# Re-slotting the work beside a feed-forward, an in-place residual, an early high band and a DMA broadcast

## What is computed

```
low = x
for 2 levels: l = dwconv(low, h_filter)[:, ::2]; h = dwconv(low, g_filter)[:, ::2]; keep h; low = l
low = linear_attention(low, 16 heads)      # q = k = elu(h)+1, v = h; num = q (k^T v), den = q . sum(k) + 1e-6
for 2 levels back: low = dwconv(repeat2(low), h_synth) + dwconv(repeat2(h), g_synth)
y = layer_norm(x + low, gamma, beta);  x1 = layernorm(x + y)
```

## Time and profile before

| what | us |
|---|---|
| median of 3 runs | 1297.83 |
| the profiled execution | 1299.54 |
| its span, first to last instruction | 1297.7 |
| prologue, to the first gate matmul | 144.4 |
| iterations 0 to 2 (with analysis) | 452.6 |
| iteration 3 | 144.5 |
| iterations 4 to 6 | 421.9 |
| iteration 7, to the last matmul | 128.0 |
| behind the last matmul | 6.3 |

### The profile page before, as it was taken

The page is one execution under the profiler, slowest core; times in us unless marked ns, Lnnn a source line. Parts: engine busy times, 40 slices in busy tenths (PEclk is TensorE's granted clock), DMA queues, the critical chain, the costliest instruction groups (busy, mean ns, idle before and its releaser), DMA issues.

```text
span 1297.7 us, 19451 instructions
## 1 busy us (share of the span) xinstructions
PE 1245.1 (96%) x6000; PEld 641.1 (49%) x6000; DVE 979.8 (76%) x1921; ACT 688.3 (53%) x1427; POOL 363.7 (28%) x794
## 2 busy tenths in 40 slices
PE   8979899989999899989999999999999999999998
PEld 6858454445444444445544444444444444444443
DVE  7878699977999599994998479955997389945231
ACT  6753563467545773467634664466444663466332
POOL 0022332144131441234330441234131433043101
PEclk9998899999999999999999999999999999999999
DMA  8980520017000240004100130014000400010000
GB/s 257 257 210 17 155 91 25 9 44 234 16 33 6 73 142 17 26 26 140 64 34 1 59 129 25 17 34 145 16 32 19 151 25 32 0 57 10 25 9 33
DMA packets 47269, 87.36 MB, mean 67 GB/s; under 512 B 8400, under 2 KB 24016, under 8 KB 46304
## 3 DMA queue, kind: packets, MB, share of 16 engines
q1 hardware_dynamic: 45472, 81.81, 19.1%
q0 software_dynamic: 1728, 4.72, 2.2%
HBM read 66.04 MB, written 25.19 MB: 70 GB/s over the span
## 4 chain that ended last, share of the span: by engine, by line
PE 42%; issue 21%; DVE 17%; ACT 9%; POOL 8%; DMA 3%; DVEq 0%; POOLq 0%; ACTq 0%; SPq 0%
PE ps_up L575 6%; PE ps_up L576 6%; PE ps_gate L575 6%; PE ps_gate L576 6%; PE ps_down L593 5%; PE ps_down L594 5%; DVE low L1195 3%; DVE hid L1550 3%; POOL rs L1118 2%; DMA q_scratch<-keys 2%; DVE s_chan L1195 2%; DVE h_f L1563 2%; DVE l L1195 2%; PE ps_y L559 1%; ACT junk L1030 1%
## 5 line engine op out<-in xcount | busy, mean ns | idle before, releaser
L575 PE MATMUL ps_gate<-x_hi,w 128*128 128x512 f16 x768 | 292.1, 380 | 2.6 <-DVE x_lo L1358 2.0
L593 PE MATMUL ps_down<-w,hid 128*128 128x512 f16 x768 | 292.6, 381 | 0.0
L575 PE MATMUL ps_up<-x_hi,w 128*128 128x512 f16 x768 | 291.9, 380 | 0.7 <-DVE h_f L1563 0.2
L594 PE MATMUL ps_down<-w,hid 128*128 128x512 f16 x768 | 292.4, 381 | 0.0
L576 PE MATMUL ps_gate<-x_lo,w 128*128 128x512 f16 x768 | 292.1, 380 | 0.0
L576 PE MATMUL ps_up<-x_lo,w 128*128 128x512 f16 x768 | 291.6, 380 | 0.0
L1563 DVE SCALAR_TENSOR_TENSOR h_f<-ps_up,h_f 128x512 f32<-128x512 f32 x192 | 130.7, 684 | 148.2 <-ACT h_f L1048 88.0
L1048 ACT ACTIVATE h_f<-ps_gate 128x512 f32<-128x512 f32 x192 | 111.6, 585 | 90.1 <-PE ps_gate L576 90.0
L1040 ACT ACTIVATE hid<-h_f 128x512 f16<-128x512 f32 x192 | 119.7, 623 | 72.1 <-DVE h_f L1563 71.6
L1550 DVE TENSOR_TENSOR hid<-h_f,hid 128x512 f16<-128x512 f32 x192 | 143.5, 747 | 3.3 <-ACT hid L1040 1.5
L575 PEld LDWEIGHTS ps_up<-x_hi,w 128*128 128x128 f16 x768 | 75.3, 98 | 94.0 <-DVE h_f L1563 3.4
(11 more groups left out here) (249 smaller groups left out, 1896.0 us busy)
## 6 DMA issues: line engine op xcount, KB each, us to landing
xt<-x_tok SPq DMA_DIRECT2D x64, 256.0 KB, 2.7
out<-z SPq DMA_DIRECT2D x64, 256.0 KB, 2.0
xa<-x_chan SPq DMA_DIRECT2D x28, 515.0 KB, 5.7
xb<-x_chan SPq DMA_DIRECT2D x7, 2060.0 KB, 8.2
w<-weights POOLq DMA_DIRECT2D x12, 384.0 KB, 7.4
q_in<-q_scratch SPq DMA_DIRECT2D x7, 518.0 KB, 8.2
h_in<-h_scratch SPq DMA_DIRECT2D x7, 518.0 KB, 9.2
h_scratch<-h SPq DMA_DIRECT2D x7, 512.0 KB, 10.8
```

The source lines that it names most:

```text
L575: pe.matmul(ps_gu[k % 2][g][:, :], w, x1_hi[:, b, c, :], start=(c == 0), stop=False)
L593: pe.matmul(ps_d[t % 2][:, :], h_hi[:, k, t * P:(t + 1) * P], w, start=(k == 0), stop=False)
L594: mm = pe.matmul(ps_d[t % 2][:, :], h_lo[:, k, t * P:(t + 1) * P], w, start=False, stop=(k == NH - 1))
```

## The change

Five things are done together.

1. The table is split in single operations, each with its own slot. On DVE `high1` and `low1` become three steps (p, k) of two taps, `band2`, `synth1a`, `synth1b` two parts each, `synth2` a high and a low part, `norm2` a `centre` and a rest; on ACT and TensorE the steps keep their names. The residual's `z_mean`, `square`, `z_scale`, `normalise` and `store` are steps of the table now too; those of block 0 run on into block 1. ACT has no early and late group any more.
2. `z` is gone: DVE writes the residual in place in `x1`, the squares go to `x1_hi` as scratch, and the store reads `x1`. `norm1` on ACT waits for the store of the tile that it overwrites; DVE's residual no longer waits for a store.
3. The high band is made two slices ahead: `xb` of slice i+2 is loaded from slot (0, 13), ACT's first taps are at (1, 4) and (1, 6), DVE's taps at (1, 13.5) to (1, 16). Iteration 0 does slice 1 (FIRST) as well. `h1` and `kvt` have memory of their own.
4. 1/den is spread by DMA: `dens` is four matmuls of 32 columns, each to its own 32 rows of `ps_y`; DVE works on 128 rows; SP issues four DMAs that copy 4 rows of `den` to 128 rows of `att` (four buffers). The `spread` matmul and ACT's copy are gone, also in the prologue.
5. The loops: iterations 0, 1 and 6 are written out; only 4 and 5 are a loop.

The core of the diff:

```diff
-    (1, 11): [(NEXT, "norm1", 2), (NEXT, "norm1q", 2), (NEXT, "normx", 0), (NEXT, "norm2", 1), (NEXT, "normq", 1)],
-    (1, 12): [(NEXT, "normx", 1), (NEXT, "norm2", 2), (NEXT, "normq", 2), (ANA, "band2", 3)],
-    (1, 12.5): [(NEXT, "norm1", 3), (NEXT, "norm1q", 3)],
-    (1, 13): [(NEXT, "norm3", 0), (NEXT, "normx", 2), (NEXT, "norm2", 3), (NEXT, "normq", 3)],
-    (1, 14): [(NEXT, "norm3", 1), (NEXT, "normx", 3)],
-    (1, 15): [(NEXT, "norm3", 2)],
-    (1, 15.5): [(NEXT, "norm3", 3), (ANA, "exp", 0)],
...
+    (0, 2): [(LATE, "turn", 0), (ANA, "low1_taps", (0, 2)), (ANA, "low1_taps", (0, 3)), (NOW, "xbeta", 5),
+             (NEXT, "bands", 0), (ANA, "low1", 1), (NOW, "norm2", 4), (NOW, "norm1q", 5), (LATE, "turn", 1)],
+    (0, 3): [(NOW, "centre", 5), (LATE, "turn", 2), (ANA, "low1_taps", (1, 1)), (LATE, "turn", 3), (NOW, "normq", 4),
+             (NOW, "norm2", 5)],
...
+    (0, 9): [(NEXT, "synth2_high", 0), (NEXT, "synth2", 0), (NEXT, "dens", 0), (NEXT, "dens_add", 0)],
+    (0, 10): [(NOW, "norm2", 7), (NEXT, "synth1a", (1, 0))],
+    (0, 11): [(NEXT, "attend", 0), (NEXT, "attend_kv", 0)],
...
+    (0, 16): [(NEXT, "synth1b", (1, 0)), (NEXT, "synth1a", (2, 1)), (NEXT, "attend", 2), (NOW, "z_scale", (0, 0))],
+    (1, 0): [(NOW, "normalise", (0, 0)), (NEXT, "attend_kv", 2), (NOW, "normalise", (0, 1)),
+             (NEXT, "synth1a", (3, 0)), (NEXT, "synth2_high", 2)],
...
+    (1, 12): [(NEXT, "norm1q", 2), (ANA, "band2_taps", (2, 0))],
+    (1, 12.5): [(NEXT, "norm1", 3), (NOW, "store", (1, 0))],
+    (1, 13): [(ANA, "band2", 3), (NOW, "z_mean", (1, 0)), (NEXT, "centre", 2), (NEXT, "normq", 1)],
+    (1, 13.5): [(AFTER, "high1_taps", (0, 1)), (NEXT, "norm1q", 3), (NEXT, "norm2", 2), (NOW, "square", (1, 0)),
+                (NEXT, "centre", 3)],
+    (1, 14): [(NEXT, "normx", 0), (NEXT, "normq", 2), (NEXT, "norm3", 0), (AFTER, "high1_taps", (0, 2)),
+              (NOW, "z_scale", (1, 0))],
+    (1, 14.5): [(NEXT, "norm2", 3), (NEXT, "normx", 1), (NOW, "store", (1, 1)), (NEXT, "normx", 2),
+                (NOW, "z_mean", (1, 1)), (ANA, "band2_taps", (2, 1)), (NEXT, "norm3", 1), (NEXT, "normq", 3)],
+    (1, 15): [(NOW, "square", (1, 1)), (NOW, "z_mean", (1, 2)), (NEXT, "norm3", 2), (NOW, "store", (1, 2)),
+              (NOW, "square", (1, 2))],
+    (1, 15.5): [(NEXT, "normx", 3), (ANA, "band2_taps", (3, 0)), (ANA, "band2_taps", (3, 1)),
+                (NOW, "normalise", (1, 0)), (NEXT, "norm3", 3), (AFTER, "high1_taps", (0, 3))],
...
+            def dens(j, batch, _):
+                hold(sp, den_step, 2 * (j + 1))
+                for c in (2, 3, 0, 1):
+                    rows = den[c * HEAD:c * HEAD + CHUNK_HEADS, :]
+                    sp.dma_start(att[:, c, :],
+                                 rows[:, None, :].to_broadcast([CHUNK_HEADS, HEAD, QW])).then_inc(ld_att[c], 16)
...
                 for c in range(NC):
-                    mm = pe.matmul(ps_y[0:HEADS, 0:QW], z_heads[:, c, :], q_in[:, c, :], start=(c == 0),
-                                   stop=(c == NC - 1))
+                    mm = pe.matmul(ps_y[c * HEAD:(c + 1) * HEAD, 0:QW], z_heads[:, c, :], q_in[:, c, :],
+                                   start=True, stop=True)
...
                     pe.wait_ge(att_done, NC * j + c)
-                pe.matmul(ps_y[:, 0:QW], spread[:, c, :], den[:, :], start=True, stop=True)
                 pe.matmul(ps_x[:, 0:QW], kv_blocks[:, c, :], q_in[:, c, :], start=True, stop=True
...
-                        dve.wait_ge(st_out[t], 16 * (B + 1))
-                        V.scalar_tensor_tensor(out=z[:, t, :], in0=ps_d[t % 2][:, :],
+                        V.scalar_tensor_tensor(out=x1[:, b * DSUB + t, :], in0=ps_d[t % 2][:, :],
```

More of the change, by code:

```diff
@@ L65 @@
 NEXT, NOW, ANA, LATE = "next iteration", "this iteration", "analysis", "close of the former analysis"
+AFTER, FIRST = "iteration behind the next", "next iteration, in the first alone"
 BESIDE = {
[L67 to L89, removed]
@@ new lines @@
+    (0, 5): [(ANA, "band2", 0), (NOW, "xbeta", 6), (NEXT, "xbeta", 0), (NOW, "normx", 5), (NOW, "norm1", 6),
+             (NOW, "norm3", 4), (NOW, "norm1q", 6)],
+    (0, 6): [(NOW, "xbeta", 7), (NOW, "centre", 6), (FIRST, "high1", 1), (FIRST, "high1_taps", (1, 1)),
+             (FIRST, "high1_taps", (1, 2)), (FIRST, "high1_taps", (1, 3))],
+    (0, 7): [(ANA, "xa", 0), (NOW, "norm2", 6), (LATE, "blocks", 0), (NOW, "norm3", 5), (NOW, "norm1", 7),
+             (NOW, "normq", 6), (NEXT, "synth1a", (0, 0))],
@@ L345, in beside @@
                     steps[name](i + 1, batch + (1 if last and not analysis else 0), n)
+                elif which is AFTER and not (isinstance(i, int) and i >= ITERS - 2):
+                    steps[name](i + 2, batch, n)
+                elif which is FIRST and first(i):
+                    steps[name](1, 0, n)
                 elif which is ANA and analysis:
@@ L560, in norm3 @@
                 mm.then_inc(x1_turned, 1)
-            steps = {"turn": turn, "kv": kv, "dens": dens, "attend": attend, "norm1": norm1, "norm3": norm3}
+            steps = {"turn": turn, "kv": kv, "dens": dens, "attend_kv": attend, "norm1": norm1,
+                     "norm3": norm3}
             def gate_up(B, b, k):
@@ L838, in norm1q @@
                 act.wait_ge(nmean1, SUBS * j + t + 1)
+                if not (first(j) and t == 0):
+                    act.wait_ge(s_squares, SUBS * j + t)
                 nc.scalar.activation(junk[:, :], x1[:, t, :], ACT.Square, bias=rs1[:, t, 1:2],
@@ L858, in norm3 @@
                                      ).then_inc(x1_hi_ready, 1)
-            early = {"low1": low1, "band2": band2, "high1": high1, "attend": attend, "synth2": synth2,
-                     "norm1": norm1, "norm3": norm3, "turn": turn}
-            late = {"exp": exp, "norm1q": norm1q, "normq": normq, "normx": normx}
             def copy(dst, src):
@@ L1571, in body @@
                             low_half(B, k)
-                            beside(b, k, i, batch, analysis, last, steps)
                     for t in range(DSUB):
@@ L1583, in body @@
                                                ).then_inc(z_done, 1)
+                    beside(b, NH + DSUB, i, batch, analysis, last, steps)
             iterations(dve, body)
```

324 lines of the change are left out of this document (180 added, 144 removed).

## The result

The changed kernel takes **1346.45 us** (median of 4 runs, 1345.97 to 1347.93), the one before 1298.12 in the same job (4 runs, 1297.37 to 1299.98). The ratio is 1.0371, 95% interval 1.0355 to 1.0388: **slower**, where 1254 and "faster" had been predicted. The profiled execution has a span of 1344.2 us.

The account below looks back on a forecast made before the run. TensorE was taken to bound the kernel, by its own instructions and 32.3 us of stalls. From 1297.7 us, less 17.6 (spread), 25.3 (stalls) and 1.2 (prologue), came 1253.6, median 1254; 8-in-10 range 1241 to 1276.

Parts of the forecast that it names:

- The prologue: Before the iterations: spread matmul off the chain, 1.2 us less; four DMAs in place within 13.6 us, cost 0.
- rival C: The DMA is late: 3 us in the prologue, 7 x 0.7 in the slices; 1262 us, chance 0.08.
- The spread matmul: In the iterations, the spread's 0.63 us of TensorE goes in 28 places: 17.6 us less, the surest term.
- The stalls: TensorE's waits between matmuls, 32.3 us: with the new order 25.3 us go and 7 stay; bounds 32.3 and 0.
- Rival A: The stalls move to other steps instead of going; only spread and prologue are gained: 1279 us, chance 0.12.
- rival B: In `dens`, matmuls on the four column groups run at once, 11.5 us less: 1242 us, chance 0.09.
- D: Slower than before: VectorE becomes the bound at the boundary of block 0 to 1; about 1305 us, chance 0.05.
- (3): Sign: waits on `x_lo` under 3 us instead of 14.3, no stretch at clock 0.50 after the first 6 us.
- (1): Sign: 28 fewer matmul pairs of L519, attend at 0.64 us between two feed-forward matmuls.
- (4): Sign: `dens` at 1.9 us, else rival B.
- (5): Sign: the `att` DMAs land before DVE's multiply.
- (2): Sign: iterations 4 to 6 at 408 us, 0 to 2 at 427.

Follow-up runs that it names:

- experiment 2: Changed kernel with a wider mask, so each of the four DMAs copies from 32 rows instead of 4: 1240.77 us, 0.9555 of the kernel before.
- experiment 4: Changed kernel with only the DMA taken back: spread matmul (now from 128 rows) and ACT's copy restored: 1253.55 us, 0.9653 of the kernel before.
- experiment 11: Kernel before, ACT's queue alone changed: `x_hi` of norm3's tile 0 placed ahead of norm1q of tile 3: 1299.23 us, 0.9993.
- experiments 7 and 9: Kernel before, norm3 moved later in the old table: 7 moves tiles 0 and 1, 1330.1 us; 9 moves tile 1 only, 1334.02 us.
- experiment 6: Kernel before with its old table and only the DMA spread (`dens` in 32 columns), copies from 32 rows: 1295.81 us, 0.9968.

## Why the prediction was wrong

**The step that failed** is in "The prologue": "four of 132 KB, even one after another at the worse of these, are in place within the 13.6 us", and for the iterations "if the DMA is late, DVE waits a little with nothing due behind it"; bounds "0 to 3 us once. I take 0". Both halves are wrong.

*The size.* The two bounds came from loads of 256 KB and 2060 KB, which differ from this copy in the one thing that mattered, the rows on the source side. Chunk 0 landed 18.4 us after the first issue in the iterations. The distance was taken as two slots, 6.9 us; by the trace DVE was ready for the multiply 4.3 us after 1/den (206.56 - 202.23). The prologue lost 6.1 us against experiment 2 (first feed-forward matmul at 148.3 instead of 142.2). The prediction even had what it needed. The Trainium skill (DMA: Bandwidth & Descriptors, "Rules for kernel authors") has the slowest dimension set the number of DMA engines. The trace agrees: 4 of sixteen would be at most 0.25, and the share is 0.20 in the gap while the copies are alone. I priced one such copy by it, "like one of 528 KB on sixteen", and not four in a row. Without the page: an `xa` load of 515 KB lands in 5.7 us in the profile of the kernel before, and three copies at 5 to 6 us before chunk 0 is there are 15 to 17, more than twice the slack. A bound also has to be held against the narrow place (seven times), not the wide one (13.6, once).

*What stands behind it.* "TensorE needs DVE's product of slot k only two slots on" is true of the gate and up products. But the low half of slot 11, which the first down slot needs for its last matmuls, is queued behind attend of slot (0, 11). So a wait of 14.2 us on DVE became one of 14.6 on TensorE, where rival C had allowed 0.7 us a slice. Rival C named the mechanism and missed the price: 8 us against 107.9 (105.7 by the medians, 107.1 by the profiled spans). That sum is the seven blocks 0, 101.8 us longer than those of experiment 2 (92.8 against 76.4, then 14.9, 13.6, 14.9, 13.5, 14.7, 13.8), and the prologue. Of the 92.8 - 76.4 = 16.4 us, 14.6 is the gap and the rest mostly the low clock behind it.

**The steps that held**, read from experiment 2, whose steady part is 58.9 us shorter than before (1147.0 to 1088.1 between the first and last feed-forward matmul):

- *The spread matmul*: 17.6 forecast in the iterations, 23.1 measured. Its 56 matmuls are gone, and besides their 0.63 us the matmuls on both sides of the pair stand closer together. A chunk cost 1.27 us and costs 0.44, the distance of the starts around it less one matmul of 0.215 (28 chunks, all within 0.01 us of these):

```profile
227.08 0.38 PE L628 MATMUL ps_down<-w,hid 128*128 128x512 f16 x1
227.30 0.60 PE L553 MATMUL ps_x<-q_in,kv_blocks 128*128 128x259 f32 x2
227.74 0.38 PE L627 MATMUL ps_down<-w,hid 128*128 128x512 f16 x1
```

  In the prologue 1.2 was forecast, and the first feed-forward matmul is 2.2 us earlier (144.4 to 142.2); kernels with the prologue of before have it at 144.4 to 147.0, so that term is right in its sign and no more. Against experiment 4, where the spread costs 0.44 us a chunk, the DMA wins 12.8 us in all.
- *The stalls*: 25.3 forecast. Taking attend (23.1) and `dens` (9.0) from 58.9 leaves 26.8, low clock included. Iterations 4 to 6 take 402.4 us against "408", 0 to 2 take 419.5 against "427". Rival A did not come. The size held; the reason given for it, one square in front of `x_hi` on ACT, is not enough: experiment 11 takes it away and the waits on `x_lo` stay, and experiments 7 and 9, which also touch the old table in one place, make them longer.
- *`dens`*, taken as 0 with 11.5 as the bound below: **rival B was true**. The two rows, before and after, from the groups of PE by form (busy us, mean ns):

```profile
L505 PE MATMUL ps_y<-q_in,z_heads 128*16 128x259 f32 x56 | 13.5, 383 | 0.0
```

and after:

```profile
L543 PE MATMUL ps_y<-q_in,z_heads 128*32 128x259 f32 x56 | 4.5, 394 | 0.1
```

  A matmul is no shorter by itself, but seven groups of eight take 4.5 us instead of 13.5: the four column groups overlap. The Trainium skill (TensorE: Matmul & The Clock Gate, "Packing small matmuls") says that they run at once; the trace agrees. So 9.0 us of a term put at 0, where rival B had 11.5.
- *D*, DVE at the block boundary, did not show: in block 1 of iteration 0 TensorE waits 0.4 us in all, in iterations 4 to 6 it is busy but for 0.34 us. *z in place and the stores* cost nothing that can be seen.

With the DMA as I had it, the forecast and rival B gave 1242; experiment 2 has 1240.77. That is closer than the terms were, and in part luck: attend gave 5.5 us more than forecast and the stalls 1.5, `dens` 2.5 less than B had, and the runs of one kernel differ by some 3. The signs and sizes of these terms were fair; the one that was called harmless was worth 106 us. Of the tests named in the prediction, for the kernel after: (3) held for the waits (1.5 us on `x_lo` at L592) but not for the clock, which is low behind each of the seven gaps; (1) was better (attend at 0.44 us); (4) went to B; (5) failed and took (2) with it, iterations 4 to 6 taking 444.2 us, over the 415 that it had named as the sign of being wrong. One addition in the prediction is off: DVE's work in iteration 0, "69 + 67 = 139", should be 71 and 67 by the numbers ahead of it; no term hangs on it.

What the prediction took for granted besides, that the time which the spread frees on TensorE is won, is false for the old table (experiment 6: 3.8 us). It is true in the new one, which gives DVE 52 and 55 us of work in the two blocks where the old has 56 and 51, and has no late group on ACT; that these two are the reason is my reading and not tested. The parts of this change are not a sum: the DMA alone is worth 3.8 us, the rest alone 45, both 58, though `dens` in 32 columns is counted in both 3.8 and 45.

## What to carry to other kernels

Price a DMA by the number of partitions on its narrow side and by how many of its kind stand ahead of it in the queue, and hold the sum against the shortest distance between issue and first use; if a value must be spread over partitions, compute it in more rows first (here a wider mask; the `dens` matmuls of the iterations take 4.5 us in all with either), and let the DMA make only the last factor. For each wait that a change adds, read the queue of the waiting engine one step on: what stands right behind it, and who needs that. A stall in a chain over several engines moved to the next tile, or grew, in all three trials that moved one entry, so test a reading of it before building on it.
